# Attention probabilities turned by a diagonal matrix, row sums taken by VectorE's addition, rows centered only, and new orders on every engine

## The reference, cut to what matters

```python
x = x + xattn(layernorm(x), ctx)
x = x + ffn(layernorm(x))

def xattn(tl, f):                 # per batch b
    q, k = f @ Wq.T + bq, f @ Wk.T + bk
    att = softmax(q @ k.T)        # over the last axis, 512 x 512
    return tl @ att.T             # "bln,bmn->blm"

def mx_dequant(t):                # blocks of 32 along the last axis
    scale = max(max|block| / 448, 1e-30)
    return fp8(block / scale) * scale

def ffn(x):
    h = silu(mx(x) @ mx(gate).T) * (mx(x) @ mx(up).T)
    return mx(h) @ mx(down).T
```

## Time and profile before

| | us |
|---|---|
| runs of the kernel before | 630.29, 1291.2, 630.39 |
| median | 630.39 |
| the profiled execution, its own time | 629.73 |
| its span (first to last instruction or transfer) | 627.9 |
| PE busy in it | 598.2 (95%) |
| DVE busy | 491.6 (78%) |
| ACT busy | 317.0 (50%) |

### The profile page before, as it was taken

One profiled execution on the slowest core, in us unless ns is written; L12 is line 12 of the kernel. 1 busy time (PEld: TensorE's weight loads), 2 busy tenths in 40 slices (PEclk: granted clock), 3 DMA queues, 4 the chain that ended last, 5 costly groups with the idle time before them and its releaser, 6 DMA issues.

```text
span 627.9 us, 6981 instructions
## 1 busy us (share of the span) xinstructions
PE 598.2 (95%) x2560; PEld 271.3 (43%) x2560; DVE 491.6 (78%) x439; ACT 317.0 (50%) x463; POOL 56.7 (9%) x70
## 2 busy tenths in 40 slices
PE   4689897999999999999999999999999999999996
PEld 1244343444344444444444444444444444444442
DVE  5978799799889898999899997899987898222110
ACT  2999987765464554555455414625422222333311
POOL 1210210010101000200101003000000000010101
PEclk9899898999999999999999999999999999999999
DMA  8946959997898958587867205729220002777862
GB/s 347 401 108 178 279 147 236 231 229 174 185 228 209 226 125 202 142 160 164 155 135 150 68 1 103 132 67 154 48 34 2 0 1 38 131 128 124 129 122 34
DMA packets 147441, 89.91 MB, mean 143 GB/s; under 512 B 134224, under 2 KB 134352, under 8 KB 142672
## 3 DMA queue, kind: packets, MB, share of 16 engines
q1 hardware_dynamic: 142080, 63.25, 43.1%
q0 software_dynamic: 5328, 26.22, 18.9%
HBM read 25.49 MB, written 8.39 MB: 54 GB/s over the span
## 4 chain that ended last, share of the span: by engine, by line
PE 41%; issue 33%; DMA 10%; ACT 9%; DVE 2%; SPq 2%; POOL 2%; POOLq 0%; ACTq 0%; DVEq 0%
PE bank L685 30%; PE bank L699 7%; PE bank L670 3%; DMA W<-hT 3%; DMA gu_lo<-hT 3%; DMA gu_hi<-hT 2%; POOL out_y L554 1%; ACT h L896 1%; ACT hT L875 1%; ACT h L887 1%; DMA hT<-W 1%; ACT dn L907 1%; DMA gu_hi<-in_ctxT 1%; ACT hT L869 1%; SPq L357 1%
## 5 line engine op out<-in xcount | busy, mean ns | idle before, releaser
L685 PE MATMUL bank<-gu_hi,xT 128*128 128x512 f16 x1024 | 305.6, 379 | 1.5 <-DMA gu_lo<-hT 1.5
L685 PE MATMUL bank<-gu_lo,xT 128*128 128x512 f16 x512 | 194.0, 379 | 0.0
L699 PE MATMUL bank<-dn,hT 128*128 128x512 f16 x768 | 166.6, 379 | 0.0
L685 PEld LDWEIGHTS bank<-gu_hi,xT 128*128 128x128 f16 x1024 | 100.2, 98 | 123.0 <-issue 2.6
L699 PEld LDWEIGHTS bank<-dn,hT 128*128 128x128 f16 x768 | 75.1, 98 | 90.6
L980 ACT ACTIVATE silu<-bank,unscale 128x512 f32<-128x512 f32 x64 | 43.0, 679 | 93.3 <-PE bank L685 52.1
L685 PEld LDWEIGHTS bank<-gu_lo,xT 128*128 128x128 f16 x512 | 50.1, 98 | 60.3 <-issue 0.3
L1497 DVE SCALAR_TENSOR_TENSOR W<-h,W 128x2048 f16<-128x2048 f32 x10 | 22.9, 2292 | 54.1 <-DMA hT<-W 49.2
L670 PE MATMUL bank<-dn,h 128*128 128x512 f32 x128 | 59.8, 626 | 3.5 <-ACT dn L919 3.5
L1465 DVE SCALAR_TENSOR_TENSOR h<-bank,unscale,silu 128x512 f32<-128x512 f32 x64 | 46.5, 746 | 13.6 <-PE bank L685 9.3
L1006 ACT ACTIVATE W<-h 128x2048 f16<-128x2048 f32 x16 | 30.6, 1910 | 47.1 <-DMA hT<-W 26.8
(11 more groups left out here) (92 smaller groups left out, 500.9 us busy)
## 6 DMA issues: line engine op xcount, KB each, us to landing
W<-in_units SPq DMA_DIRECT2D x12, 1024.0 KB, 6.2
W<-hT POOLq DMA_DIRECT2D x12, 1024.0 KB, 6.0
h<-W POOLq DMA_DIRECT2D x6, 1024.0 KB, 6.0
h<-in_xcols SPq DMA_DIRECT2D x4, 1024.0 KB, 14.1
out_y<-y POOLq DMA_DIRECT2D x16, 256.0 KB, 5.1
gu_hi<-in_ctxT SPq DMA_DIRECT2D x4, 512.0 KB, 8.6
h<-in_xrows SPq DMA_DIRECT2D x2, 1024.0 KB, 11.8
out_y<-h SPq DMA_DIRECT2D x2, 1024.0 KB, 6.3
```

The lines of the kernel that those rows point to most:

```text
L685: last = pe.matmul(bank[:, :], xT[:, b % 2, part, k, :], w[:, c, g, j * 512:(j + 1) * 512], start=(m == 0), stop=(m == 3 * HT - 1))
L699: last = pe.matmul(bank[:, :], hT[:, r % 2, a, k, :], dn[:, w, k, :], start=(m == 0), stop=(m == 3 * IT - 1))
```

## The change

It has five parts, and new orders around them (the sixth point).

1. *The turning of probabilities.* `divide` is gone. DVE's new `weigh(b, nt)` writes a 128 x 128 diagonal matrix with the inverse sums (the identity times `rsum`), and `turn_probs` multiplies each tile by it in an ordinary f32 matmul, where it turned the tile against the identity in transpose mode.
2. *Row sums.* `add_attended` gets an `accum_out` that sums the new rows; `attended_means(b)` on DVE makes the negative mean. The copy with accumulator of ACT and the `bn_stats` of DVE are gone. ACT's `attended_variances(b)` is the square with accumulator, now for all four b.
3. *Rows only centered.* `normalize` on ACT is gone. DVE's `center(b)` subtracts the mean; the inverse deviation is multiplied into the 128 x 64 block scales in `rows_dequant(b)`.
4. *The last row tile stored plainly.* SP's `load_last` reads the 128 rows of x after attention back, ACT's `add_constant` adds the constant, DVE's `add_last(n)`, four of them, scale `down(15)` and add, and SP's `store_last` writes them. `take_down(15)` and `add_out(15)` are gone.
5. *An early exponential.* ACT begins with an exponential of four elements, and waits for one memset of POOL for it.
6. *Orders.* `products`, `rounds`, `bank_uses` and the call lists of all five engines are new. `load_unit(2)` goes ahead of the rows 2 and 3. The products (2,0) and (0,0) stand among the turns of batch 3, ahead of `attend(3, ...)`. Rows 1 are needed by the ninth product, where they were needed by the thirteenth.

The core of the diff; the lists are cut to the stretches that the prediction speaks of.

```diff
-    products = [(0, 0), (3, 0), (0, 1), (3, 1), (2, 0), (2, 1), (1, 0), (1, 1), (0, 2), (2, 2), (1, 2), (3, 2),
-                (5, 0), (5, 1), (4, 0), (3, 3), (4, 1), (4, 2), (2, 3), (4, 3), (0, 3), (6, 0), (6, 1), (6, 2),
...
+    products = [(2, 0), (0, 0), (0, 1), (2, 1), (3, 0), (3, 1), (1, 0), (1, 1), (5, 0), (4, 0), (4, 1), (4, 2),
+                (1, 2), (6, 0), (6, 1), (5, 1), (2, 2), (0, 2), (4, 3), (0, 3), (6, 2), (6, 3), (1, 3), (3, 2),
...
-    rounds = ("u0 u1 u2 u3 u4 n0 u5 n1 u6 u7 u8 u9 u10 u11 h0 n2 h1 h2 h3 h4 h5 h6 h7 h8 n3 h9 h10 h11 h12 h13 h14"
+    rounds = ("u0 u1 u2 u3 n0 u4 n1 u5 u6 u7 u8 u9 u10 u11 h0 h1 n2 h2 h3 n3 h4 h5 h6 h7 h8 h9 h10 h11 h12 h13 h14"
...
+        diagonal = [[h[:, nt, 512 + n * P:512 + (n + 1) * P] for nt in range(LT)] for n in range(2)]
...
             load_rows(1)
+            load_unit(2)
             load_rows(2)
             load_rows(3)
             load_columns(0)
             load_columns(1)
-            load_unit(2)
...
             def turn_probs(b, nt):
                 bank = take_bank(f"t{b}.{nt}")
-                pe.wait_ge(probs_ready, LT * b + nt + 1)
-                turn4(bank, [probs[b % 2][:, nt, j * P:(j + 1) * P] for j in range(HT)]).then_inc(probs_turned, 1)
+                pe.wait_ge(diagonal_ready, LT * b + nt + 1)
+                for j in range(HT):
+                    last = pe.matmul(bank[:, j * P:(j + 1) * P], probs[b % 2][:, nt, j * P:(j + 1) * P],
+                                     diagonal[b % 2][nt], start=(j == 0), stop=(j == HT - 1))
+                last.then_inc(probs_turned, 1)
...
             turn_probs(3, 0)
             turn_probs(3, 1)
+            product(2, 0)
             turn_probs(3, 2)
             turn_probs(3, 3)
+            product(0, 0)
             attend(3, 0)
...
-            def divide(b, nt):
-                act.wait_ge(rsum_ready, b + 1)
-                nc.scalar.activation(probs[b % 2][:, nt, :], probs[b % 2][:, nt, :], ACT.Copy,
-                                     scale=rsum[:, LT * b + nt:LT * b + nt + 1]).then_inc(probs_ready, 1)
...
+            def attended_variances(b):
+                act.wait_ge(ymean_ready, b + 1)
+                if b == 2:
+                    act.wait_ge(*unit_lo_done(U_ALL - 1))
+                elif b > 0:
+                    act.wait_ge(nT_in[0], 16 * b)
+                    act.wait_ge(nT_in[1], 16 * b)
+                if b >= 2:
+                    act.wait_ge(xnorm_ready, b + 1)
...
+            def weigh(b, nt):
+                dve.wait_ge(rsum_ready, b + 1)
+                if b >= 2:
+                    dve.wait_ge(probs_turned, LT * (b - 1))
+                dve.tensor_scalar(diagonal[b % 2][nt], idf, rsum[:, LT * b + nt:LT * b + nt + 1], None, ALU.mult
+                                  ).then_inc(diagonal_ready, 1)
...
-                dve.scalar_tensor_tensor(rows, bank_of(f"a{b}.{lt}")[:, :], xrstd[:, LT * b + lt:LT * b + lt + 1], rows,
-                                         ALU.mult, ALU.add).then_inc(x1_ready, 1)
+                dve.scalar_tensor_tensor(rows, bank_of(f"a{b}.{lt}")[:, :], xrstd[:, row], rows, ALU.mult, ALU.add,
+                                         accum_out=ysum[:, row]).then_inc(x1_ready, 1)
+            def attended_means(b):
+                dve.wait_ge(x1_ready, LT * (b + 1))
+                dve.tensor_scalar(nmean[:, of(b)], ysum[:, of(b)], -1.0 / H, None, ALU.mult).then_inc(ymean_ready, 1)
+            def center(b):
...
+                for lt in range(LT):
+                    cols = slice(lt * H, (lt + 1) * H)
+                    last = dve.tensor_scalar(xw_of(b)[:, cols], src[:, cols], nmean[:, LT * b + lt:LT * b + lt + 1], None,
+                                             ALU.add)
+                last.then_inc(xnorm_ready, 1)
...
             def rows_dequant(b):
                 xw = xw_of(b)
                 rounded(f"n{b}")
+                dve.wait_ge(rstd_ready, b + 1)
+                each_row = rstd[:, of(b)].unsqueeze(2).broadcast_to([P, LT, NB // LT])
+                rows = xscale[:, :].rearrange("p (t n) -> p t n", t=LT)
+                then(dve.tensor_tensor(rows, rows, each_row, ALU.mult))
...
+            def add_last(n):
+                dve.wait_ge(odown_ready, RT)
+                dve.wait_ge(last_ready, 1)
+                dve.wait_ge(down_ready, RT)
+                cols = slice(n * P, (n + 1) * P)
+                dve.scalar_tensor_tensor(last_out[:, cols], bank_of(f"d{RT - 1}")[:, cols],
+                                         odown[:, (RT - 1) % 4, n:n + 1], last_x[:, cols], ALU.mult, ALU.add
+                                         ).then_inc(last_summed, 1)
```

More of the change, by code:

```diff
@@ L631, in _ @@
             add_out(14)
-            add_out(15)
         @block.tensor
         def _(pe):
-            def turn4(dst, tiles):
-                for j, t in enumerate(tiles):
-                    last = pe.matmul(dst[:, j * P:(j + 1) * P], t, idf, is_transpose=True,
-                                     start=(j == 0), stop=(j == 3))
-                return last
             def take_bank(key):
@@ L736, in _ @@
             turn_probs(1, 3)
+            energies(2, 1)
+            energies(2, 2)
+            energies(2, 3)
             attend(1, 0)
@@ L746, in _ @@
             turn_probs(2, 3)
+            energies(3, 0)
+            energies(3, 1)
             energies(3, 2)
@@ L786, in _ @@
             product(1, 3)
+            product(3, 2)
+            product(3, 3)
             product(5, 2)
@@ L793, in _ @@
             down(0)
+            product(2, 3)
+            down(1)
             product(8, 0)
@@ L796, in _ @@
             product(8, 2)
+            product(8, 3)
             product(9, 0)
-            product(8, 3)
-            down(1)
+            product(9, 1)
+            product(9, 2)
             product(10, 0)
+            product(9, 3)
             product(10, 1)
+            product(10, 2)
+            product(10, 3)
             product(11, 0)
@@ L921, in take_probs @@
                                      ACT.Copy).then_inc(at_ready, 1)
-            def attended_stats(b):
-                act.wait_ge(x1_ready, LT * (b + 1))
-                if b == 1:
-                    act.wait_ge(*rows_lo_done(0))
-                for lt in range(LT):
-                    cols = slice(lt * H, (lt + 1) * H)
-                    last = nc.scalar.activation(early_xw[:, cols], X[b][:, cols], ACT.Copy,
-                                                accum_out=ysum[:, LT * b + lt:LT * b + lt + 1])
-                act.wait_ge(act_step, own.done(last))
-                act.wait_ge(act_step, own.done(
-                    nc.scalar.activation(nmean[:, of(b)], ysum[:, of(b)], ACT.Copy, scale=-1.0 / H)))
+            def attended_variances(b):
[7 more added lines that the diff above has]
+                    act.wait_ge(xnorm_ready, b + 1)
+                squares = xparts_of(b).rearrange("p a n -> p (a n)").bitcast(F32)
                 for lt in range(LT):
@@ L1127, in _ @@
-            unit_magnitude(6)
-            silu_of(2, 1)
+            silu_of(0, 1)
+            rows_hi(1)
+            unit_lo(4)
+            silu_of(2, 1)
+            silu_of(3, 0)
+            rows_lo(1)
+            unit_rescale(5)
+            unit_magnitude(5)
+            unit_rescale(6)
+            silu_of(3, 1)
+            silu_of(1, 0)
+            unit_magnitude(6)
+            unit_hi(5)
+            silu_of(1, 1)
+            silu_of(5, 0)
             unit_lo(5)
-            rows_hi(1)
@@ L1502, in _ @@
             unit_scale(0)
+            unit_power(0)
             unit_reduce(1)
[L1504 removed]
             unit_largest(1)
+            unit_round(0)
+            unit_dequant(0)
+            row_max(0, 0)
+            unit_power(1)
             unit_scale(1)
[L1507 to L1508 removed]
+            unit_reduce(2)
+            unit_largest(2)
             row_max(0, 1)
@@ L1554, in _ @@
             row_max(3, 3)
-            add_attended(1, 3)
             add_attended(2, 0)
-            unit_round(4)
+            rows_lo(0)
+            unit_reduce(4)
             row_sum(3)
-            unit_dequant(4)
+            weigh(3, 0)
+            weigh(3, 1)
+            weigh(3, 2)
+            weigh(3, 3)
+            unit_largest(4)
+            unit_scale(4)
+            unit_power(4)
             add_attended(2, 1)
```

797 lines of the change are left out of this document (387 added, 410 removed), and 8 rows, old and new, of the table products.

## The result

The changed kernel takes 638.14 us (median of 4 runs, 637.17 to 638.35). The kernel before, run beside it, takes 630.91 (median of four; one of them, 1291.2, is a slow run that the ratio leaves out, the others took 630.29 to 631.43). The ratio is 1.0115 with an interval of 1.0095 to 1.0135: slower by 1.15%, inside the 2% of "same". The prediction was 624.4 us with a range of 616 to 636. The result lies 13.7 us above the forecast and 2.1 above the range.

What follows compares the result with a forecast made beforehand. The feed-forward stage was taken as bound by PE's matmuls alone. 120.0 us beside the products + 497.7 of products + 4.9 of tail = 622.6 span, + 1.83 around it = 624.4 us; range 616 to 636.

Steps and rivals of the forecast that it cites:

- 82.4 + 14.0 + 23.6 = 120.0: PE's time beside the products: 82.4 us of 128x512 matmuls, 14.0 of diagonal turns, 23.6 not worked.
- The tail: After the last matmul: four DVE additions 1.2 us, plain store 3.7; 4.9 us instead of 6.0.
- the walk: Following each engine's list with its durations: first attend starts at 46.3 us, last attend ends near 129.
- the new front: Before the first attend: DVE's list runs without a hole from 15.1 us, first diagonal at 38.7, attend at 46.3.
- The rival of DVE late with the diagonals: `weigh` behind load waits, 2.5 us late in two batches, low clock: adds 5 to 8, 629 to 632; chance 0.14.
- PE's own work: In the attention stage: turns 0.109 us apart, two records each, +7.0 us on PE; attend 0 from 46.3 to 60.0.
- The prices of the new DVE work: DVE durations: `weigh` 0.22 us each, bounded by 0.190 and 0.684; `center` 0.42 each, between 0.19 and 0.75.
- The 0.1 each: Extra DVE time for the `accum_out` of each `add_attended`: 0.1 us, 1.6 in all, bounds 0 and 3.2.
- So nothing there costs: Supply of rows and units behind the attends: all arrive in time, and the old 1.5 us wait goes.
- forecast margin of 8: Rows 1 turned near 153 us, needed by the ninth product at 161.5: margin 8 us.
- stated margin of 6 us: Rows 2 landed near 300 us, needed at product 33, at 306.
- The added 2.3 us at rows 0: Allowance in PE's not-worked time for rows 0 landing 1 to 2 us late and low clock once.

Runs made afterwards that it cites:

- e1: Changed kernel with POOL's first power (`first_norm(0)`) moved behind the third maximum: 629.75 us, ratio 0.9981 to the kernel before.
- e2: Changed kernel with DVE's `unit_power(2)` moved behind the first four diagonals, POOL's order kept: 631.9 us, ratio 1.0023 to the kernel before.
- e5: On top of e1, the chain of rows 2 moved ahead of hidden 1's work in the ACT, DVE and POOL queues: 627.65 us, ratio 0.9945.
- e6: On top of e1, SP's load of unit 5 issued behind the turn of unit 2's second half: 630.42 us, ratio 0.9983.
- e7: On top of e1, ACT divides the probabilities again, PE turns in transpose mode, DVE weighs no diagonals: 630.6 us, ratio 0.9986.

## Why the prediction was wrong, by its own steps

The forecast of the span was 622.6; it came out 636.4, 13.8 more. The sum had 82.4 + 14.0 + 23.6 = 120.0 beside the two products (10.4), so the attends were to end at 130.4. They end at 138.70: +8.3. From there to the last matmul are 493.9 us where 497.7 - 10.4 = 487.3 stood: +6.6. The tail is 3.8 for 4.9: -1.1. 8.3 + 6.6 - 1.1 = 13.8. The first 8.3 are 9.0 for the first attend (55.34 against 46.3) and 0.7 for the stretch of the attends (83.36 against 82.7), less the 1.4 by which the sum (130.4) had been put above the walk (129).

- *The step that failed* is in the new front: "From 15.1 us ... its list runs without a hole", with row sums at 38.4 and the first diagonal at 38.7. They came at 44.36 and 44.57. The walk gave every DVE instruction its duration and took for granted that the two powers of 0.6 us in it had their input. POOL got no walk. In the trace of before the same 5.9 us of "issue" stood ahead of POOL's third maximum, but there DVE's power stood behind the row sums and 2.3 us of unit scaling (`unit_scale(2)`, L1425) and lost 0.84 (the lines below). The change moved the power ahead of both and uncovered the wait. e1 and e2 show it from both sides: with the hole gone the diagonals come at 38.38 to 38.6 and the first attend at 46.95, 0.65 from the forecast's 46.3. Of the 9.0 us that the first attend was late, 5.9 are the diagonal (44.57 against 38.7) and 2.4 the low clock behind the wait, which the walk had not either.

```profile
37.76 0.38 POOL L520 PARTITION_ALL_REDUCE umax<-smax  x1 [5.86 <-issue]
```

```profile
38.17 0.15 DVE L1331 TENSOR_SCALAR pow<-umax 128x1 int32<-128x1 int32 x1 [0.84 <-POOL umax L520]
```

- The Trainium skill ("GPSIMD Engine Reference", Instruction dispatch) says that the first call to freshly loaded code on POOL pays some 6 us which no instruction of the profile shows. The traces agree on the size, 5.6 to 8.0 us behind the configuration where the input was there, and they show it for every change between maximum and power or product, not for a first call alone. This was the rule that spoke against the change, and the prediction did not weigh it.
- *The rival of DVE late with the diagonals* (629 to 632) named the right engine and victim, but other waits (for loads), of 2.5 us in each of two batches, where one wait of 5.9 stood in the first.
- *PE's own work* was right: turns 0.109 apart, attends of 13.90, and from the first attend to the end of the last 83.36 us, where the walk had 46.3 to 129, 82.7.
- *The prices of the new DVE work* were right or high: `weigh` four in 0.88 us (0.20 apart; taken 0.22), `center` four in 1.67 (0.40 apart; taken 0.42, though the terms named for it, 0.19 and half of 448/512 of 0.684, add up to 0.49). The accumulator's read on DVE is a record of 82 ns, and the next addition starts as if it weren't there: `add_attended` follow each other at 0.67 to 0.68. The 0.1 each was too much, and harmless. The Trainium skill's count of two instructions ("VectorE: DVE Perf Modes", Two Vector instructions with no wait between them) shows as two records, but not as time.
- *"So nothing there costs"* was wrong by 4.3 us of waits, 0.3 at a `down`, and 1.4 of low clock; 0.6 of the 6.6 is not assigned to any row. Rows 1 came in time with about half the forecast margin of 8: their turns, issued at 159.05 and 161.73, had landed at 166.1, and the ninth product started at 170.66. Rows 2 had not. Their stated margin of 6 us (306 against 300) was an estimate without a walk of the lists, and they were 20 us later than it, 8.3 of them because all is shifted. e5 shortens the wait and the time falls, so it was real.
- *The added 2.3 us at rows 0* was near for the mended kernel: e1 waits 1.74 at (2,0) ahead of the last attend. Its 0.86 at (0,1) and 1.14 near 180 come behind it, where the forecast had none.
- *The tail* was forecast as -1.1 and is -2.2: the plain store of 256 KB lands in 2.1 us. I had bounded it from 2 to 5.1 and taken 3.7; the lower end was right. The Trainium skill ("SBUF — State Buffer", The DMA setup-cost knee) gives 2 us plus the bytes at 436 GB/s, an estimate of 2.6 us for it, nearer than the row of the accumulating store.

With the mended POOL order the forecast of 624.4 is 5.4 us from the 629.75 measured. With rows 2 mended as well, it is 3.3 from 627.65. What remains is seen in e5's waits: 0.99 at (2,0), 1.00 at (0,1), 0.69 at 179, 1.21 at (8,0). That a version without them reaches 624 has not been tried.

## What to carry to other kernels

Walk the lists of all engines that feed the one you count, the idle ones too. POOL was busy for 8% of the span and decided 8 us. A group of waits on "issue" at an engine is a price like any other; when a change moves its consumer forward, this price comes onto the path. Put POOL instructions of one kind together, and look at the queue's configuration instructions to see each change of code. What a change costs is counted from there: with the next input 7.6 us or more behind the configuration it cost nothing here, with the input already there up to 8.0. And before shortening one link of a chain (a turn, a division), look at what the chain meets next: twice here (e6, e7) the gain was handed to the following wait.

## What the runs showed of the hardware that was not expected

- A change of code on POOL is paid every time POOL goes from the maximum to a power or back: 5.6 to 8.0 us from the configuration instructions to the start in 44 changes, 10.4 to 12.0 in the six near 15 us.
- It runs beside the wait for the input: in the 32 changes whose input came 7.6 us or more behind the configuration nothing of it was left (0.08 to 0.14 us).
- An f32 matmul of 128 columns against a diagonal takes twice the time of one in transpose mode (0.218 against 0.109), and two records instead of one. Its weight loads, 201 ns each by the groups, stayed hidden beside matmuls at that spacing.
- A plain store of 256 KB took 2.1 us from issue to landing, where the accumulating one of the same size takes 5.0 to 5.1.
